# Deformable convolution after an edge-update block: patches of 14 by 8 pixels for two groups of 4 by 4 sample positions

## The chip, the cores and the metric

One core of a Trainium2 chip. The metric is the device time of one execution in microseconds (us), the median of several. TensorE (PE) multiplies matrices into PSUM, VectorE (DVE) and ScalarE (ACT) move and change data, GpSimd (POOL) does too but reaches SBUF only, SyncE (SP) issues DMAs.

## The reference

`x` is (2, 128, 128, 128), float32. Two layers are each added to their input:

```python
x = x + _L0_conv_ref(_gn(x), Wa, ba, Wb, bb, Wg, bg, Wo, bo)   # sigmoid(gate) * (a @ b), then @ Wo
x = x + _L1_conv_ref(_gn(x), w_off, b_off, w_def)

def _L1_conv_ref(x, w_off, b_off, w_def):
    x = jax.nn.relu(x)
    offset = conv(x, w_off, 3x3, padding 1) + b_off       # 18 channels: dy, dx for each of 9 taps
    py, px = base_y + off[:, :, 0], base_x + off[:, :, 1]  # 9 sample positions a pixel
    samp = _bilinear_gather(x, py, px)                     # zero outside the image
    return einsum('bckhw,ock->bohw', samp, w_def)
```

The change is in the second layer.

## The kernel before, in words

**First stage (to about 330 us).** 64 groups of rows go through layer one; the sum goes to DRAM as `x1_pad`, with a margin. Constant tables are loaded by SP in small pieces on the way.

**Band stage.** The image is cut into 64 bands of 8 rows by 64 columns. Sampling is a matrix product: for a window of 5 centre columns, all sample positions lie in a patch of 14 by 9 = 126 pixels (offsets up to 2 pixels). The patch, turned so that pixels lie on partitions, is PE's stationary operand (`zT`), and the moving one is `weights` (126 pixels by 9 taps by 40 positions): the product of a vertical and a horizontal hat function of the distance of each pixel to each position. A band has 66 centre columns of 8 (528 positions a tap), 14 windows and 13 steps. Each band passes these stages, and each engine runs them in the order of the table `ORDER`, in which a letter names the stage and a fixed lead in bands:

- `h` (3 bands ahead): ACT normalises the near pixels (L971) and rounds them to f16 (L959), DVE makes the low parts `z_lo` (L1324). `O`: PE convolves them to offsets (L824: nine products with `z_hi`, nine with `z_lo`), which leaves four partial sums on four groups of partitions; ACT adds the bias and takes them out (L982, `offs4`). `P`: DVE casts them to f16 (L1288) and subtracts (L1291), the split. `Q`, `locate`: PE selects and adds the partial sums and the constants for every (patch row, tap) and (patch column, tap) (L762 high, L764 low, for each axis), ACT takes the absolute value (L991, `dist`). `G`: DVE makes `hats` (L1299). `H`: ACT issues the stores of the hats to DRAM (L997). `R`: DVE reduces the reach (L1304).
- SP, `spread_hats`: each third (3 taps) of a band's hats is read back and broadcast, hat_y over the 9 patch columns, hat_x over 12 of the patch rows, into `hy_all` and `hx_all` (L564, 108 partitions by 1536 columns each). There is one buffer of each, so the loads of a third wait until POOL's three products of the band before with that third are done.
- `k` (1 ahead): POOL multiplies `hy_all` and `hx_all` into `weights` (L1570, nine products of 512 columns a band). `weights` has two buffers; the first product of a band waits until all sampling of the band before last is done.
- `z`, `T` (2 and 1 ahead): ACT makes the patches (L948), PE turns the 14 windows four at a time (L796), ACT and DVE copy them out in turns (L1015, L1334).
- `s`: PE samples (L778, 9 by 40 columns a step; float32, so each product is two passes), ACT copies the step to `samples_hi` in f16 (L1005), DVE makes `samples_lo` (L1314). There are three PSUM banks, so step p waits until the low parts of step p - 3 are done. Step 0 waits for all of the band's weights.
- `c` (1 behind): PE convolves (L750: three products of 512 columns a tap), DVE adds x (L1349), SP stores y.

## Time and profile before

| | |
|---|---|
| median of 3 runs (lowest, highest) | 1680.81 us (1674.68, 1682.14) |
| profiled execution: own time; span | 1692.53; 1690.7 us |
| PE busy; VectorE; ScalarE; GpSimd | 1543.5; 1096.4; 990.7; 941.8 us |
| TensorE's mean granted clock | 0.962 of full |
| DMA, mean over the span | 211 GB/s |
| hy_all and hx_all loads | 192 each, 648.0 KB each |
| chain that ended last, largest shares | DMA 42%, PE 23%, POOL 16% |

The span is what the trace covers; the own time of the profiled execution holds a little more, and both lie above the median of the runs. Busy PE time comes from modelled ends of pipelined matmuls, so the start of the next instruction tells the price of one better than its duration does. A reader takes the distance between starts where nothing waits. In rows, `L` is the line of the kernel, the first number the start, the second the length, and brackets give the idle time before and what ended it.

### The profile page before, as it was taken

What the parts mean: (1) busy time and instruction counts of PE and PEld (TensorE: products, weight loads), DVE (VectorE), ACT (ScalarE), POOL (GpSimd) and SP (SyncE); (2) the same over time, 40 slices, a digit from 0 to 9 for tenths busy, and PEclk for the clock granted to TensorE, in tenths of its full rate; (3) what the DMA queues carried; (4) which work ended last, traced back from release to release, by engine and by line L of the source; (5) the groups of instructions that cost most, each with busy time, mean ns of one, the idle gap of its engine ahead of it and who ended that gap; (6) DMA issues with size and microseconds to landing.
All of it is one profiled execution on the core that took longest, in us unless ns stands there. A gap on an engine that the chain in (4) does not pass through costs nothing.

```text
span 1690.7 us, 24883 instructions
## 1 busy us (share of the span) xinstructions
PE 1543.5 (91%) x8339; PEld 910.3 (54%) x8340; DVE 1096.4 (65%) x1964; ACT 990.7 (59%) x1564; POOL 941.8 (56%) x747
## 2 busy tenths in 40 slices
PE   6999999748998999989999999899999999889997
PEld 4777777514554555444554555455445554445554
DVE  6888888645666676565665666657556656556663
ACT  3555555435665666665666666557556666556662
POOL 4555555535565565555555655565556655556652
PEclk9999999858999999999999999999999999999999
DMA  5334333347777777777777777877787778777762
GB/s 149 116 117 116 116 115 112 120 145 250 235 253 247 244 259 236 235 230 236 244 230 240 237 256 246 235 239 240 238 249 247 267 230 247 219 235 251 253 243 68
DMA packets 145855, 356.90 MB, mean 211 GB/s; under 512 B 10875, under 2 KB 77976, under 8 KB 145752
## 3 DMA queue, kind: packets, MB, share of 16 engines
q1 hardware_dynamic: 131032, 328.46, 62.8%
q10 hardware_dynamic: 14720, 27.14, 4.6%
q8 instruction: 56, 0.92, 0.2%
q14 instruction: 47, 0.39, 0.1%
HBM read 292.42 MB, written 63.13 MB: 210 GB/s over the span
## 4 chain that ended last, share of the span: by engine, by line
DMA 42%; PE 23%; POOL 16%; issue 11%; DVE 3%; SPq 2%; ACT 1%; ACTq 0%; POOLq 0%; DVEq 0%
DMA hx_all<-hat_x 38%; POOL weights L1570 10%; PE bank L778 9%; PE pair L750 7%; POOL samples_hi L1519 4%; DMA hat_x<-hats 4%; PE pair L824 3%; SPq L564 2%; POOL rstd L1494 1%; PE pair L796 1%; POOL samples_lo L1506 1%; DVE hats L1299 1%; PE bank L796 1%; PE pair L762 1%; PE pair L764 1%
## 5 line engine op out<-in xcount | busy, mean ns | idle before, releaser
L1570 POOL TENSOR_TENSOR weights<-hy_all,hx_all 126x512 f32<-126x512 f32 x576 | 759.4, 1347 | 570.0 <-DMA hx_all<-hat_x 530.3
L1314 DVE SCALAR_TENSOR_TENSOR samples_lo<-bank,samples_hi 128x360 f16<-128x360 f32 (+1 forms) x832 | 434.1, 536 | 432.1 <-ACT samples_hi L1005 419.0
L778 PE MATMUL bank<-weights,zT 126*128 126x360 f32 (+1 forms) x1792 | 637.3, 474 | 78.1 <-POOL weights L1570 74.7
L1005 ACT ACTIVATE samples_hi<-bank 128x360 f16<-128x360 f32 (+1 forms) x832 | 385.4, 475 | 431.4 <-PE bank L778 405.0
L778 PEld LDWEIGHTS bank<-weights,zT 126*128 126x128 f32 x1792 | 314.8, 196 | 239.1 <-POOL weights L1570 79.7
L750 PE MATMUL pair<-samples_hi,w_hi 128*128 128x512 f16 x576 | 221.7, 385 | 1.3 <-DVE samples_lo L1314 1.3
L750 PE MATMUL pair<-samples_hi,w_lo 128*128 128x512 f16 x576 | 220.0, 382 | 0.0
L750 PE MATMUL pair<-samples_lo,w_hi 128*128 128x512 f16 x576 | 219.3, 381 | 0.0
L1506 POOL TENSOR_TENSOR samples_lo<-samples_hi,samples_lo 128x512 f16<-128x512 f32 x64 | 74.2, 1159 | 130.8 <-ACT samples_lo L909 130.7
L900 ACT ACTIVATE samples_hi<-pair,nbias,rstd 128x512 f32<-128x512 f32 x64 | 49.8, 778 | 148.5 <-PE pair L649 97.0
L948 ACT ACTIVATE z<-raw,norm_band 128x1764 f32<-128x1764 f32 (+3 forms) x80 | 132.1, 1671 | 0.0
L971 ACT ACTIVATE abg_space<-raw,norm_band 128x660 f32<-128x660 f32 (+2 forms) x74 | 101.9, 1391 | 17.2 <-DMA raw<-x_pad 11.8
L750 PEld LDWEIGHTS pair<-samples_hi,w_lo 128*128 128x128 f16 x576 | 57.2, 99 | 99.2 <-issue 69.4
L1299 DVE TENSOR_SCALAR hats<-dist 128x1024 f32<-128x1024 f32 x64 | 64.7, 1011 | 61.7 <-ACT dist L991 61.7
L824 PE MATMUL pair<-z_hi,woff 128*64 128x512 f16 x576 | 87.5, 412 | 15.9 <-ACT z_hi L959 15.9
L1015 ACT COPY zT<-pair 126x512 f32<-126x512 f32 x128 | 75.0, 586 | 37.1 <-PE pair L796 32.7
L750 PEld LDWEIGHTS pair<-samples_hi,w_hi 128*128 128x128 f16 x576 | 56.8, 99 | 71.4 <-issue 5.3
L750 PEld LDWEIGHTS pair<-samples_lo,w_hi 128*128 128x128 f16 x576 | 56.1, 97 | 70.8 <-issue 3.3
L991 ACT ACTIVATE dist<-pair 128x1024 f32<-128x1024 f32 x64 | 65.6, 1025 | 37.1 <-PE pair L764 37.1
L1519 POOL TENSOR_TENSOR samples_hi<-weights,all_o 128x512 f32<-128x512 f32 x64 | 81.5, 1275 | 0.0
L796 PEld LDWEIGHTS pair<-ident,z 128*126 128x126 f32 x512 | 64.8, 142 | 26.3 <-issue 2.1
L796 PE MATMUL pair<-ident,z 128*126 128x128 f32 x512 | 78.1, 276 | 0.0
(138 smaller groups left out, 1920.5 us busy)
## 6 DMA issues: line engine op xcount, KB each, us to landing
hy_all<-hat_y SPq DMA_DIRECT2D x192, 648.0 KB
hx_all<-hat_x SPq DMA_DIRECT2D x192, 648.0 KB
raw<-x_pad SPq DMA_DIRECT2D x68, 276.0 KB, 14.6
x_pad<-hy_all SPq DMA_DIRECT2D x64, 276.0 KB, 3.7
weights<-in_x SPq DMA_DIRECT2D x64, 256.0 KB, 3.0
out<-y SPq DMA_DIRECT2D x32, 512.0 KB, 13.5
hat_y<-hats ACTq DMA_DIRECT2D x64, 252.0 KB
hat_x<-hats ACTq DMA_DIRECT2D x64, 162.0 KB
```

The costliest lines, as they stand in the source:

```text
L750: mm = nc.tensor.matmul(bank[B_CONV], w_part[:, k, :], part[:, u, k, k % 3 * BR:k % 3 * BR + BW], start=(k == 0 and (w_part, part) == (w_h ...
L778: mm = nc.tensor.matmul(sampled_step(n, p)[:, :, c0 - first:c1 - first], zT[0:WPIX, u * WINDOWS + w, :], weights[0:WPIX, u, :, c0:c1], sta ...
L796: mm = nc.tensor.transpose(bank[B_ZT[g % 2]][0:WPIX, (w % 4) * P:(w % 4 + 1) * P], z[:, u, w].rearrange("p r c -> p (r c)"), ident[:])
L824: mm = nc.tensor.matmul(bank[B_OFF][at:at + width, :].rearrange("p (w r) -> p w r", r=BR), woff[:, k, 0:width], pixels[:, kx:kx + UW, ky:k ...
L948: done = nc.scalar.activation(z[:, u, :, rows, :], patches, ACT.Relu, bias=norm_band[:, 1].rearrange("p b n -> p (b n)")[:, n:n + 1], scal ...
L971: done = nc.scalar.activation(z_near[:, :, r0:r1], raw[:, src:src + r1 - r0, left:left + UW + 2].rearrange("p r w -> p w r"), ACT.Relu, bi ...
L1005: nc.scalar.activation(samples_hi[:, u, :, c0:c1], sampled_step(n, p), ACT.Copy).then_inc(samples_ready, 1)
L1299: nc.vector.tensor_scalar(hats[:], dist[:], -1.0, 0.0, ALU.add, ALU.min).then_inc(hats_ready, 1)
L1314: nc.vector.scalar_tensor_tensor(out=samples_lo[:, u, :, c0:c1], in0=sampled_step(n, p), scalar=1.0, in1=samples_hi[:, u, :, c0:c1], op0=A ...
L1506: nc.gpsimd.tensor_tensor(xT_lo[:], xT[:], xT_hi[:], ALU.subtract).then_inc(xT_lo_ready, 1)
L1519: nc.gpsimd.tensor_tensor(x_bo[:, s % 2, :].rearrange("p (f w) -> p f w", f=GC), xg[:, s, :].rearrange("p (f w) -> p f w", f=GC), all_o[:] ...
L1570: nc.gpsimd.tensor_tensor(weights[0:WPIX, u, k, at:at + BW], hy_all[0:WPIX, k, :], hx_all[0:WPIX, k, :], ALU.mult).then_inc(weights_ready, 1)
```

## The change

The patch becomes 14 by 8 pixels (112 partitions), a window 4 centre columns. Each patch serves two groups of 4 by 4 positions, the upper and lower half of the band, so every product samples 2 x 9 x 16 = 288 columns; a band has 17 windows and 16 steps. `hats`, `weights`, `hy_all`, `hx_all` and the banks hold the halves one behind the other. Each half needs 8 of the 14 patch rows, so a load writes 64 partitions. A band's loads are six pieces (half, 3 taps) in two DMAs each, 768 columns wide, and POOL makes one product of 3 x 256 columns for each. hat_y lies in DRAM twice per row (`COPIES`). The stores of the hats move from ACT's queue to SP's, behind the loads, and are six. The partial sums are first added two and two: ACT takes out partitions 64 on with bias (`offs_far`), DVE adds those from 0 on (`offs_sum`, a new instruction), and high and low parts then lie in one tensor (`offs_parts`), so that `locate` is one product an axis. `ORDER` is rewritten. The rest of the diff, left out below, lays constants out for this (eight more small loads in the first stage) and keeps the path for far offsets.

```diff
-BR, WC, UW = 8, 5, 64
+BR, WC, UW = 8, 4, 64
+HR = BR // 2
...
-CW = CENTERS * BR
+CW = CENTERS * HR
-WIN = WC * BR
+WIN = WC * HR
-NEAR_R = BR + 2 * REACH
+NEAR_R = HR + 2 * REACH
+COPIES = 2
...
+HALF = BW // 2
+CHUNK = TROWS * HALF
+PIECES = 2 * TAPS // TROWS
...
-            "h0 s0 s1 s2 k0 h1 c0 c1 T0 k1 s3 s4 z0 z1 O0 k2 s5 s6 P0 c2 c3 T1 k3 s7 s8 c4 k4 c5 s9 Q0 "
-            "c6 k5 G0 T2 s10 k6 H0 c7 k7 s11 c8 T3 k8 s12 R0").split()]
+            "h0 s0 s1 s2 k0 h1 c0 c1 s3 s4 T0 k1 z0 z1 O0 s5 s6 P0 k2 c2 c3 s7 s8 T1 c4 k3 c5 s9 s10 "
+            "Q0 k4 c6 G0 T2 s11 s12 c7 k5 T3 s13 s14 c8 T4 s15 R0").split()]
...
                 sp.wait_ge(*hats_landed(n))
-                for g in range(TROWS):
-                    wait(sp, weights_ready, TAPS * (n - 1) + TROWS * (g + 1))
...
+                for i in range(PIECES):
+                    h, g = divmod(i, TROWS)
+                    wait(sp, weights_ready, PIECES * (n - 1) + i + 1)
...
+                    sp.dma_start(
+                        hy_flat[rows, columns],
+                        hat_y[n % AHEAD, g, top * COPIES:(top + NEAR_R) * COPIES, h]
...
+            def store_hats(n):
+
+                sp.wait_ge(hats_ready, n + 1)
+                for h in range(2):
+                    columns = slice(h * HALF, (h + 1) * HALF)
+                    for copy in range(COPIES):
+                        sp.dma_start(
...
+                            hats[0:Y_ROWS, 0, columns]).then_inc(hat_out[n % AHEAD], 16)
+                    sp.dma_start(
...
                 if n + 2 < BANDS:
                     spread_hats(n + 2)
+                if n + AHEAD < BANDS:
+                    store_hats(n + AHEAD)
...
                 for axis in range(2):
-                    nc.tensor.matmul(pairs[0][:, axis, :], select[:, axis, :],
-                                     offs_hi[:], start=True, stop=False)
-                    mm = nc.tensor.matmul(pairs[0][:, axis, :], select[0:CONST_AT, axis, :],
-                                          offs_lo[0:CONST_AT, :], start=False, stop=True)
+                    mm = nc.tensor.matmul(pairs[0][:, axis, :], select[:, axis, :],
+                                          offs_parts[:], start=True, stop=True)
...
                 dve.wait_ge(off_evicted, n + 1)
+                wait(dve, off_split, n)
+                nc.vector.scalar_tensor_tensor(
+                    out=offs_sum[0:SUMS, :], in0=bank[B_OFF][0:SUMS, :],
+                    scalar=unscale[0:SUMS, OFF:OFF + 1], in1=offs_far[0:SUMS, :],
+                    op0=ALU.mult, op1=ALU.add).then_inc(off_summed, 1)
...
-            def weigh(n, u, k):
+            def weigh(n, u, i):
+
+                pool.wait_ge(hat_in[i], 32 * n + 32)
+                if i == 0:
                     wait(pool, sampled, STEPS * (n - 1))
...
+                             ap=[first.ap[0], [CW + HR, TROWS], [1, HALF]])
+                nc.gpsimd.tensor_tensor(to, hy_all[0:WPIX, i * TROWS:(i + 1) * TROWS, :],
+                                        hx_all[0:WPIX, i * TROWS:(i + 1) * TROWS, :],
+                                        ALU.mult).then_inc(weights_ready, 1)
```

VectorE, from the low parts `z_lo` to the hats. Before:

```order
L1324 TENSOR_TENSOR z_lo<-abg_space,z_hi 128x660 [waits z_hi_ready]
L1314 SCALAR_TENSOR_TENSOR samples_lo<-bank,samples_hi 128x9x40 [waits samples_ready] x4
L1288 CAST offs_hi<-offs 114x512 [waits located,off_evicted]
L1291 TENSOR_TENSOR offs_lo<-offs,offs_hi 114x512 [waits off_high]
L1334 COPY zT<-bank 126x512 [waits sampled,z_turned]
L1314 SCALAR_TENSOR_TENSOR samples_lo<-bank,samples_hi 128x9x40 [waits samples_ready] x3
L1299 TENSOR_SCALAR hats<-dist 128x1024 [waits hat_out0,dist_ready]
```

The same place after the change:

```order
L1379 TENSOR_TENSOR z_lo<-abg_space,z_hi 128x660 [waits z_hi_ready]
L1369 SCALAR_TENSOR_TENSOR samples_lo<-bank,samples_hi 128x18x16 [waits samples_ready] x4
L1337 SCALAR_TENSOR_TENSOR dist<-pair,unscale,dist 50x512 [waits off_split,off_evicted]
L1343 CAST offs_parts<-dist 50x512 [waits located,off_summed]
L1346 TENSOR_TENSOR offs_parts<-dist,offs_parts 50x512 [waits off_high]
L1369 SCALAR_TENSOR_TENSOR samples_lo<-bank,samples_hi 128x18x16 [waits samples_ready] x2
L1389 COPY zT<-bank 112x512 [waits sampled,z_turned]
L1369 SCALAR_TENSOR_TENSOR samples_lo<-bank,samples_hi 128x18x16 [waits samples_ready] x2
L1354 TENSOR_SCALAR hats<-dist 128x1024 [waits hat_out1,dist_ready]
```

The split has a sum ahead of it, and the low parts of steps 7 and 8 now stand directly behind it, ahead of the copy of windows.

PE, the sampling steps ahead of `locate`. Before, from the sixth product of the convolution on:

```order
L750 MATMUL pair<-samples_lo,w_hi 128x512
L778 MATMUL bank<-weights,zT 128x360 [waits lows_ready]
L762 MATMUL pair<-offs_hi,select 128x512 [waits dist_ready,off_split]
L764 MATMUL pair<-offs_lo,select 128x512
L762 MATMUL pair<-offs_hi,select 128x512
L764 MATMUL pair<-offs_lo,select 128x512
L750 MATMUL pair<-samples_hi,w_hi 128x512
```

After:

```order
L799 MATMUL pair<-samples_lo,w_hi 128x512
L828 MATMUL bank<-weights,zT 128x288 [waits lows_ready] x2
L812 MATMUL pair<-offs_parts,select 128x512 [waits dist_ready,off_split]
L812 MATMUL pair<-offs_parts,select 128x512
L799 MATMUL pair<-samples_hi,w_hi 128x512
```

Two steps, 9 and 10, stand ahead of `locate` where one stood, and the second of them needs the low parts of step 7.

## Rows read from the trace of the kernel before

**Rows 1.** Windows view: us, busy us (instructions) per engine, PEclk, DMA share, GB/s.

```profile
400.00:1040.00 640.00, 604.39 (x2850) 323.99 (x2850) 405.31 (x661) 400.87 (x640) 369.32 (x281) 0.98 0.78 242
```

**Rows 2.** Chain that ended last, 800 to 845 us: start, us, what.

```profile
822.86 16.92 DMA hx_all<-hat_x
```

**Rows 3.** Waits view, PE and POOL, 400 to 1680: us, times, longest.

```profile
PE bank L778 <- POOL weights L1570: 71.3, 31, 7.9
...
POOL weights L1570 <- DMA hx_all<-hat_x: 486.8, 172, 9.9
```

**Rows 4.** Source view of L1349, the addition of x: xcount, min/median/max ns, first, last start.

```profile
L1349 DVE SCALAR_TENSOR_TENSOR y<-pair,unscale,raw x74: 274/742/744, 421.7 to 1683.9; 128x512 f32<-128x512 f32 x54, 128x320 f32<-128x320 f32 x6, 128x192 f32<-128x192 f32 x6, 128x64 f32<-128x64 f32 x4
```

**Rows 5.** Timeline of PE, 1108.5 to 1129: start, us, engine line op xcount.

```profile
1108.29 1.32 PE L824 MATMUL pair<-z_hi,woff 128*64 128x512 f16 x9
...
1111.66 0.38 PE L750 MATMUL pair<-samples_hi,w_hi 128*128 128x512 f16 x1
...
1112.96 0.60 PE L796 MATMUL bank<-ident,z 128*126 128x128 f32 x4
1113.39 1.38 PE L778 MATMUL bank<-weights,zT 126*128 126x360 f32 x4
1114.61 0.38 PE L750 MATMUL pair<-samples_hi,w_hi 128*128 128x512 f16 x1
...
1121.20 3.08 PE L778 MATMUL bank<-weights,zT 126*128 126x360 f32 x10
1124.12 0.38 PE L750 MATMUL pair<-samples_hi,w_hi 128*128 128x512 f16 x1
...
1127.16 1.32 PE L824 MATMUL pair<-z_hi,woff 128*64 128x512 f16 x9
```

**Rows 6.** Timeline of PE, then of POOL, around 441 us.

```profile
440.24 2.20 PE L778 MATMUL bank<-weights,zT 126*128 126x360 f32 x8
...
441.33 3.74 POOL L1570 TENSOR_TENSOR weights<-hy_all,hx_all 126x512 f32<-126x512 f32 x3 [5.04 <-PE bank L778]
```

**Rows 7.** Source views of L1545 and L1570: xcount, min/median/max ns.

```profile
L1545 POOL TENSOR_TENSOR w_lo<-weights,w_hi x1: 2381/2381/2381, 307.6 to 307.6; 128x1152 f16<-128x1152 f32 x1
L1545 POOL TENSOR_TENSOR woff<-weights,woff x1: 496/496/496, 309.9 to 309.9; 128x162 f16<-128x162 f32 x1
...
L1570 POOL TENSOR_TENSOR weights<-hy_all,hx_all x559: 1254/1273/1972, 399.7 to 1660.4; 126x512 f32<-126x512 f32 x187
```

**Rows 8.** Timeline, 1120.5 to 1141, then source views of L1291 and L1314.

```profile
1122.74 0.61 DVE L1314 SCALAR_TENSOR_TENSOR samples_lo<-bank,samples_hi 128x432 f16<-128x432 f32 x1 [0.19 <-ACT samples_hi L1005]
...
1124.83 4.35 POOL L1570 TENSOR_TENSOR weights<-hy_all,hx_all 126x512 f32<-126x512 f32 x3 [6.37 <-DMA hx_all<-hat_x]
...
1125.92 0.88 DVE L1324 TENSOR_TENSOR z_lo<-abg_space,z_hi 128x660 f16<-128x660 f32 x1
...
1130.64 4.35 POOL L1570 TENSOR_TENSOR weights<-hy_all,hx_all 126x512 f32<-126x512 f32 x3 [1.46 <-DMA hx_all<-hat_x]
...
1131.68 0.51 DVE L1288 CAST offs_hi<-offs 114x512 f16<-114x512 f32 x1
...
1132.22 1.64 DVE L1291 TENSOR_TENSOR offs_lo<-offs,offs_hi 114x512 f16<-114x512 f32 x1
...
L1291 DVE TENSOR_TENSOR offs_lo<-offs,offs_hi x64: 691/693/1762, 345.6 to 1621.5; 114x512 f16<-114x512 f32 x64
...
L1314 DVE SCALAR_TENSOR_TENSOR samples_lo<-bank,samples_hi x832: 515/533/609, 382.7 to 1676.7; 128x360 f16<-128x360 f32 x154, 128x432 f16<-128x432 f32 x13
```

**Rows 9.** Timeline of PE at its first sampling step.

```profile
380.59 2.17 PE L778 MATMUL bank<-weights,zT 126*128 126x360 f32 x3 [3.36 <-POOL weights L1570]
```

**Rows 10.** Timelines of ScalarE's and SP's queues, first band's hats and a later load.

```profile
350.70 0.27 ACTq L997 DMA_DIRECT2D hat_x<-hats  x1
...
353.65 0.85 SPq L564 DMA_DIRECT2D hy_all<-hat_y  x1
...
1131.46 0.76 SPq L564 DMA_DIRECT2D hy_all<-hat_y  x1
```

More of the change, by code:

```diff
@@ L241, in preact_conv_kernel @@
         parts = sb("parts", [P, BW], BF16)
-        offs, rest = hy_all[0:NOFF, 0], hy_all[0:NOFF, 1]
-        row_in, row_z, row_zT = (hy_all[:, 2, i * P:(i + 1) * P] for i in range(3))
-        far_dist, far_hats, far_weights = hx_all[:, 0:2], hx_all[:, 2:4], weights[:, 1, 0, 0:BW]
-        samples = weights[:, 0, :, 0:BW]
+        offs, rest = hy_far[0:NOFF, 0], hy_far[0:NOFF, 1]
+        row_in, row_z, row_zT = (hy_far[:, 2, i * P:(i + 1) * P] for i in range(3))
+        far_dist, far_hats = hx_far[:, 0:2], hx_far[:, 2:4]
+        samples, far_weights = (weights[:, i].rearrange("p k c -> p (k c)")[:, 0:TAPS * BW]
+                                .rearrange("p (k c) -> p k c", k=TAPS) for i in range(2))
+        far_weights = far_weights[:, 0]
         in_f32 = sem("in_f32")
@@ L398, in sampled_step @@
             first, end = step_columns(p)
-            return (bank[B_S[(STEPS * n + p) % 3]][:, 0:TAPS * (end - first)]
-                    .rearrange("p (k c) -> p k c", k=TAPS))
+            return (bank[B_S[(STEPS * n + p) % 3]][:, 0:2 * TAPS * (end - first)]
+                    .rearrange("p (k c) -> p k c", k=2 * TAPS))
         def by_column_tap(tile):
@@ new lines, in store_hats @@
+            def store_hats(n):
+                sp.wait_ge(hats_ready, n + 1)
+                for h in range(2):
+                    columns = slice(h * HALF, (h + 1) * HALF)
+                    for copy in range(COPIES):
+                        sp.dma_start(
+                            hat_y[n % AHEAD].rearrange("g (r o) h c -> (g r) o h c", o=COPIES)
+                            [:, copy, h].rearrange("a (k c) -> a k c", k=TROWS),
+                            hats[0:Y_ROWS, 0, columns]).then_inc(hat_out[n % AHEAD], 16)
+                    sp.dma_start(
+                        hat_x[n % AHEAD].rearrange("r g h c -> (r g) h c")
+                        [:, h].rearrange("a (k c) -> a k c", k=TROWS),
+                        hats[0:X_ROWS, 1, columns]).then_inc(hat_out[n % AHEAD], 16)
@@ L571, in _ @@
             sp.wait_ge(hats_cleared, 2)
-            spread_hats(0)
-            spread_hats(1)
+            for n in range(AHEAD):
+                store_hats(n)
+                if n + 1 < AHEAD:
+                    spread_hats(n)
             for n in range(BANDS + 2):
@@ L769, in sample @@
                 if p == 0:
-                    wait(pe, weights_ready, TAPS * (n + 1))
+                    wait(pe, weights_ready, PIECES * (n + 1))
                 if p % 4 == 0:
@@ L991, in distances @@
                 nc.scalar.activation(dist[:], pairs[0][:], ACT.Abs).then_inc(dist_ready, 1)
-            def store_hats(n, u, _):
-                wait(act, hats_ready, n + 1)
-                for axis, rows in enumerate((Y_ROWS, X_ROWS)):
-                    act.dma_start(hat_rows[axis][n % AHEAD].rearrange("g r (k c) -> (g r k) c", k=TROWS),
-                                  hats[0:rows, axis, :]).then_inc(hat_out[n % AHEAD], 16)
             def copy_samples(n, u, p):
@@ L1344, in add_x1 @@
                 whole = min(BR, RING * RB - at)
-                for r0, r1, src in ((0, whole, at), (whole, BR, 0)):
-                    if r0 == r1:
-                        continue
-                    added = nc.vector.scalar_tensor_tensor(
-                        out=y[:, b % 2, :].rearrange("p (r w) -> p r w", r=BR)[:, r0:r1,
-                                                                              left:left + UW],
-                        in0=bank[B_CONV].rearrange("p (w r) -> p r w", r=BR)[:, r0:r1],
-                        scalar=unscale[:, DEF:DEF + 1],
-                        in1=raw[:, src:src + r1 - r0, MARGIN + left:MARGIN + left + UW],
-                        op0=ALU.mult, op1=ALU.add)
+                to = y[:, b % 2, :].rearrange("p (r w) -> p r w", r=BR)
+                of = bank[B_CONV].rearrange("p (h w r) -> p h r w", h=2, r=HR)
+                for h in range(2):
+                    cut = min(max(whole - h * HR, 0), HR)
+                    for r0, r1 in ((0, cut), (cut, HR)):
+                        if r0 == r1:
+                            continue
+                        src = (at + h * HR + r0) % (RING * RB)
+                        added = nc.vector.scalar_tensor_tensor(
+                            out=to[:, h * HR + r0:h * HR + r1, left:left + UW],
+                            in0=of[:, h, r0:r1], scalar=unscale[:, DEF:DEF + 1],
+                            in1=raw[:, src:src + r1 - r0, MARGIN + left:MARGIN + left + UW],
+                            op0=ALU.mult, op1=ALU.add)
                 added.then_inc(y_ready, 1)
```

150 lines of the change are left out of this document (85 added, 65 removed).

## Prediction, made before the changed kernel ran

> **What bounds the kernel now.** I read the busy time by stretch first, then the chain, the waits, and one band instruction by instruction. In the band stage TensorE (PE) is busy 604 of 640 us while VectorE, ScalarE and GpSimd (POOL) stand at 405, 401 and 369 [rows 1]: PE is nearly the bound. Yet the chain that ended last runs for bands on end through a load of hx_all, 16.92 us of it in a band, and the products that wait for it [rows 2]. The waits join the two: POOL waits 486.8 us for hx_all, in 172 pieces, and hands on only 71.3 us to PE, in 31 [rows 3]. The mean band is (1683.9 - 421.7) / 63 = 20.03 us [rows 4]. A band without a wait for POOL takes PE from 1108.29 to 1127.16, 18.87 us [rows 5]. So loads that come late cost 1.16 us a band, the waits and the lower clock in some bands (0.98 granted on the mean [rows 1]) together. **No more than 73 us can be had this way, and what the new band costs comes off it.**
>
> **PE's own stream.** The sampling products have 9 x 528 = 4752 columns a band before and 18 x 264 = 4752 after, so that price stays; the convolution has the same 27 products of 512 columns. Added: three window turns, at (1113.39 - 1112.96) / 4 = 0.11 each, +0.33 [rows 5]. Removed: two of four 512-column products of `locate`; six such products take 1112.96 - 1111.66 = 1.30, so -0.43 [rows 5]. At the seam of two bands the last step and the first three of the next take 1124.12 - 1121.20 = 2.92 us [rows 5]; their columns (eight full passes at (1114.61 - 1113.39) / 4 = 0.30 each, two to a step, and two short ones, 0.12) fill some 2.53. PE waits 0.39 there: the third step's bank is freed 1.59 us after the last step's end. The new last step has the same 432 columns, but the two steps ahead of the third shrink from 0.60 to 0.48 each, so the wait grows to 0.63: +0.24. Sum 18.87 + 0.33 - 0.43 + 0.24 = 19.0 us for a PE that waits for nothing else.
>
> **The loads.** A band's loads shrink from 6 x 108 rows of 6144 bytes (4.0 MB) to 12 x 64 rows of 3072 (2.4 MB), and each of six pieces is freed by its own product. In a band of 20 us the transfers that took 17 us for a third of 4.0 MB, with the rest beside it, have time to land: I count POOL's wait for loads at nothing. What covers it is a whole band between the issue of a piece and its use.
>
> **What is late next: POOL against VectorE.** POOL then starts its products as soon as the buffer is free, 0.37 us after the last sampling step (440.24 + 0.72 = 440.96 to 441.33) [rows 6], and runs all six in a row. Call that step's end zero. One product of 3 x 256 columns is not in the trace. The one of 512 takes 1273 ns. A product with one half-size operand takes 496 ns for 162 columns and 2381 for 1152, thus 1.90 ns a column and 0.19 us fixed [rows 7]. Floor: 1.27 + 256 x 1.90 = 1.76 us; ceiling: 1.5 x 1.27 = 1.91. I take 0.19 + 1.5 x 1.08 = 1.81, nearest to the row of the same types, less 0.04 of overlap (three stand in 3.74 us, not 3.82 [rows 6]): 1.775 apart. Whether three rows of 256 in one product cost more than one of 768 no row shows; the ceiling holds 0.05 us for each of the two. The Trainium skill, page GPSIMD Engine Reference, section Elementwise — side-by-side cycle accounting, counts about 2.6 cycles of 1.2 GHz an element for a product of two inputs; an estimate by it is 1.83 us, 0.1 us more a band and 6 us more in all.
>
> POOL and VectorE get in each other's way. The cast of the split began at 1131.68 during a product that ended at 1131.91, and ended 0.28 after it; the subtraction behind it took 1.64 us instead of 0.69 [rows 8]. The other way round, `z_lo` at 1125.92 stretched the three products from 1124.83 on to 4.35 instead of 3.74, by 0.61 [rows 6, 8]. The subtraction's median is 693 ns and its longest 1762 [rows 8], so in most bands no product was in its way; now one is in every band. `z_lo` asks at 1125.92 - 1121.92 = 4.0, or 3.8 with shorter copies ahead, near the end of the second product. So POOL ends at 0.37 + 6 x 1.775 + 0.04 + 0.61 = 11.67. The cast came at 1131.68 - 1121.92 = 9.76 [rows 8]; shorter steps ahead take 0.24 off and the new sum of partial offsets, one input in PSUM like `y`'s 0.74, adds as much as that [rows 4] (bounds: nothing, if VectorE were idle there, and 0.74 + 0.2 for latency). It asks at 10.26, after the sixth product has begun at 9.86. **It waits for that product.** Cast done at 11.95, subtraction 11.99 to 12.68, then the low parts of step 7, which may begin 0.08 before the end: 533 ns for 360 columns and 609 for 432 make 0.46 for 288 [rows 8], to 13.06. Step 10 needs that bank, 0.17 us later (the seam shows 1123.35 to 1123.52): **13.23**. Its place in PE's order is 12.35 (seam to the third step's end 2.07; then seven steps at 0.48, six taps of the convolution at 0.65, two turns of four windows at 0.44, and the offsets' convolution 1111.66 - 1108.29 less two steps, 2.15), so PE waits 0.9 us. From there to the band's end stand five steps of 0.48 and the last of 0.72, three taps 1.94, nine turns 0.98 and `locate` 0.43: 6.49 with the rounding. Band: 13.23 + 6.49 = **19.72**. With products from floor to ceiling (1.72 to 1.87 apart) 19.4 to 20.0; at the ceiling the cast slips in ahead of the sixth product and only the subtraction waits.
>
> **Outside the bands.** PE's first sampling step waited 3.36 us for POOL's first products [rows 9]; smaller pieces end that: -3.4. Eight more small loads in the set-up, at the 0.76 us that SP takes for a load [rows 10], come while SP is ahead of the first groups: 0, up to +6. Two halves of the last addition, extra copy of windows, longer patches for ScalarE: VectorE and ScalarE have 35% free, and every wait on them falls inside the 0.9 us that PE waits anyway; were that gone they would cost some 0.2.
>
> **Sum.** 63 x (19.72 - 20.03) = -19.5, and -3.4: -23 us against the profiled execution (span 1690.7, its own time 1692.5, 0.7% over the median). On the median of 1680.8 that is **1658 us**. For the products' bounds: 1638 to 1677. A measurement of this kernel can tell about 0.5% (8 us) from no change.
>
> **Rivals.**
> 1. *PE alone is the bound*: the cast gets through, because products are shorter or start earlier than I think. 19.0 a band, 1680.8 - 65 - 3 = 1613. For it: PE has no other wait in a clean band. Against: the products would have to stand 1.63 apart, below my floor. 0.12.
> 2. *SP's queue becomes the loop* (the slower side). Stores leave ScalarE and go to SP, six instead of two. The loop is: stores landed, twelve loads issued, stores issued, landed. A load's issue takes 0.76, and the first loads began 353.65 - 350.97 = 2.7 us after the stores' issue [rows 10]. With stores at the 0.76 of a load the loop is 9.1 + 4.6 + 2.7 and 0.9 for `raw` and `y`: 17.3, under the band. At the 0.27 of the old store it is 14.3. From 1.2 us a store it decides; at 1.3 it is 20.5 and the time 1680.8 + 30 - 3 = 1707. For it: stores in rows of 3 x 256 are new here, so no row prices them. Against: 2.4 us to spare. 0.15.
> 3. *The loads are hidden no better*: shorter rows, the second copy of hat_y's rows and 648 store rows instead of 207 eat the gain, POOL still waits, and the change does not do what it says. Then the band stays near 20.03, with the new cost of PE (+0.13) 1680.8 + 8 - 3 = 1685. For it: the transfers are shared out in order. Against: 40% fewer bytes at the same 242 GB/s [rows 1]. 0.15.
>
> **Chances.** Forecast 0.58 (0.50 of it faster, 0.08 same), PE alone 0.12 (faster), SP 0.15 (0.13 slower, 0.02 same), loads 0.15 (0.10 same, 0.05 slower). Faster 0.62, same 0.20, slower 0.18. Range 1630 to 1700: it reaches most of the way to both outer cases and leaves out about 0.1 on each side.
>
> **What would show it.** Right: POOL's wait for hx_all falls from 487 us to near nothing and its wait for PE's sampling takes the place; six products in a row from 0.4 to 11.7 us after the last step; cast and subtraction of the split behind the sixth; PE waiting about 0.9 us for samples_lo at step 10 and 0.6 at step 2 in every band; the granted clock near 1.00 in the bands. Wrong: a product far from 1.8 us, a split that ends before the sixth product, waits of POOL for loads, or SP's loads issued later than the products that free their place.

## The result, and the profile after

The changed kernel takes 1656.14 us (median of 4 runs, 1655.2 to 1658.35), the one before 1679.61 (4 runs, 1674.68 to 1682.14): a ratio of 0.9866, 95% interval 0.984 to 0.9891. It is faster, by 1.3%, and 2 us from the forecast. As shown below, part of that closeness is luck. Ratios and intervals in this document use only the runs within 1.5% of the fastest of their kernel. 54 more runs of the kernel before, made beside the experiments below, have a median of 1673.3 us, and six of them lie below 1656.1: against those the change is worth 1.0%, and not in every execution. The profiled execution has its own time of 1655.2 and a span of 1653.1 us.

The windows view of the same stretch as [rows 1]: span of the stretch, then busy us and instructions of PE, PEld, DVE, ACT and POOL, then clock, DMA share and GB/s.

```profile
400.00:1040.00 640.00, 627.58 (x3160) 363.79 (x3159) 501.71 (x845) 441.13 (x790) 366.65 (x195) 1.00 0.63 183
```

PE is busy 628 of 640 us in place of 604, at a granted clock of 1.00 in place of 0.98, and the DMA engines move 183 GB/s in place of 242. The waits view, 400 to 1640 us (us in total, times, longest), answers to [rows 3]:

```profile
POOL weights L1629 <- PE bank L828: 513.8, 61, 8.8
...
PEld pair L874 <- DVE z_lo L1379: 36.4, 58, 0.7
...
POOL weights L1629 <- DMA hx_all<-hat_x: 6.6, 3, 5.4
```

GpSimd waited 486.8 us for `hx_all`; now 6.6, and its wait for TensorE's sampling has taken the place. TensorE waits for no weights in this stretch. The loads are off the path, as forecast.

One band of TensorE, with the rows that say where it stands (timeline: start, length, what, idle time before and its releaser). It answers to [rows 5].

```profile
1099.87 1.61 PE L874 MATMUL pair<-z_hi,woff 128*64 128x512 f16 x9
...
1102.47 1.24 PE L828 MATMUL bank<-weights,zT 112*128 112x288 f32 x4
...
1107.55 1.45 PE L828 MATMUL bank<-weights,zT 112*128 112x288 f32 x4
1108.84 0.60 PE L812 MATMUL pair<-offs_parts,select 119*128 119x512 f16 x2
...
1114.15 1.87 PE L828 MATMUL bank<-weights,zT 112*128 112x288 f32 x8
1116.31 0.75 PE L828 MATMUL bank<-weights,zT 112*128 112x288 f32 x2 [0.29 <-DVE samples_lo L1369]
1116.90 0.38 PE L799 MATMUL pair<-samples_hi,w_hi 128*128 128x512 f16 x1
```

GpSimd, two bands (timeline): the distance of the starts, 19.82 us, is the band, and the six products take 11.3. The last row is from the source view of all 384 products: shortest, median and longest, in ns.

```profile
1095.37 11.34 POOL L1629 TENSOR_TENSOR weights<-hy_all,hx_all 112x768 f32<-112x768 f32 x6 [8.49 <-PE bank L828]
1115.19 7.76 POOL L1629 TENSOR_TENSOR weights<-hy_all,hx_all 112x768 f32<-112x768 f32 x4 [8.49 <-PE bank L828]
...
L1629 POOL TENSOR_TENSOR weights<-hy_all,hx_all x384: 1799/1822/2476, 368.3 to 1617.3; 112x768 f32<-112x768 f32 x192
```

The second row is cut off at the window's end. VectorE in the same band (timeline), to be read beside GpSimd's products, which end at 1095.37 + 11.34 = 1106.71:

```profile
1098.96 2.50 DVE L1379 TENSOR_TENSOR z_lo<-abg_space,z_hi 128x660 f16<-128x660 f32 x1
...
1104.57 0.73 DVE L1337 SCALAR_TENSOR_TENSOR dist<-pair,unscale,dist 50x512 f32<-50x512 f32 x1
1105.33 1.65 DVE L1343 CAST offs_parts<-dist 50x512 f16<-50x512 f32 x1
1107.02 0.69 DVE L1346 TENSOR_TENSOR offs_parts<-dist,offs_parts 50x512 f16<-50x512 f32 x1
1107.73 0.82 DVE L1369 SCALAR_TENSOR_TENSOR samples_lo<-bank,samples_hi 128x288 f16<-128x288 f32 x2
```

The cast begins at 1105.33 and ends at 1106.98, 0.27 after the sixth product. With no product beside it, it takes 0.42 (shown below). `z_lo` takes 2.50 in place of 0.8. Counted from the end of the last sampling step of the band before (1114.15 + 0.72 less a band, 1095.05), the forecast chain stands like this:

| us after the last step | forecast | measured |
|---|---|---|
| first product starts | 0.37 | 0.32 |
| sixth product ends | 11.67 | 11.66 |
| cast ends | 11.95 | 11.93 |
| subtraction ends | 12.68 | 12.66 |
| low parts of step 7 | 13.06 | about 13.1 |
| step 10 starts (0.48 before 1108.84) | 13.23 | 13.31 |
| step 10's own place in PE's order | 12.35 | 12.98 (1107.55 + 0.48) |
| from step 10 to the band's end | 6.49 | 6.51 |
| band | 19.72 | 19.82 |

### The profile page after: what moved, and what is told of

Its sections match the earlier page's. It is cut to its first block, busy times and chain, and to the rows that moved or that the text cites. A ratio compares the mean times of both kernels' runs of the same rounds, so it can differ in the third digit from the quotient of the medians.

```text
span 1653.1 us, 26938 instructions
## 1 busy us (share of the span) xinstructions
PE 1555.0 (94%) x8787; PEld 972.4 (59%) x8788; DVE 1271.9 (77%) x2283; ACT 1044.2 (63%) x1820; POOL 907.9 (55%) x555
## 4 chain that ended last, share of the span: by engine, by line
PE 60%; issue 13%; DVE 11%; POOL 7%; ACT 6%; SPq 2%; DMA 1%; POOLq 0%; DVEq 0%; ACTq 0%
PE bank L828 25%; PE pair L799 17%; PE pair L874 9%; POOL samples_hi L1577 4%; DVE samples_lo L1369 4%; PE pair L846 4%; DVE offs_parts L1343 3%; ACT samples_hi L1050 3%; PE bank L846 2%; PE pair L812 2%; ACT dist L1034 2%; DVE dist L1337 2%; POOL rstd L1552 1%; ACT z L999 1%; POOL samples_lo L1564 1%
## 5 line engine op out<-in xcount | busy, mean ns | idle before, releaser
L1629 POOL TENSOR_TENSOR weights<-hy_all,hx_all 112x768 f32<-112x768 f32 x384 | 724.3, 1922 | 556.4 <-PE bank L828 513.8
L828 PE MATMUL bank<-weights,zT 112*128 112x288 f32 (+1 forms) x2176 | 630.3, 410 | 25.9 <-DVE samples_lo L1369 23.2
L1050 ACT ACTIVATE samples_hi<-bank 128x288 f16<-128x288 f32 (+1 forms) x1024 | 409.5, 416 | 365.5 <-PE bank L828 337.8
L1369 DVE SCALAR_TENSOR_TENSOR samples_lo<-bank,samples_hi 128x288 f16<-128x288 f32 (+1 forms) x1024 | 445.9, 463 | 225.8 <-ACT samples_hi L1050 219.6
L828 PEld LDWEIGHTS bank<-weights,zT 112*128 112x128 f32 x2176 | 370.8, 190 | 206.4 <-DVE samples_lo L1369 127.8
L1379 DVE TENSOR_TENSOR z_lo<-abg_space,z_hi 128x660 f16<-128x660 f32 x64 | 148.4, 2319 | 5.3 <-ACT z_hi L1010 2.2
L999 ACT ACTIVATE z<-raw,norm_band 128x1904 f32<-128x1904 f32 (+3 forms) x80 | 131.2, 1660 | 0.0
L1060 ACT COPY zT<-pair 112x512 f32<-112x512 f32 (+1 forms) x192 | 91.9, 479 | 29.1 <-PE pair L846 23.5
L1343 DVE CAST offs_parts<-dist 50x512 f16<-50x512 f32 x64 | 96.2, 1504 | 2.2
L846 PE MATMUL pair<-ident,z 128*112 128x128 f32 x576 | 95.8, 276 | 0.0
```

What stands on the lines that cost most here:

```text
L828: mm = nc.tensor.matmul(sampled_step(n, p)[:, :, c0 - first:c1 - first], zT[0:WPIX, u * WINDOWS + w, :], weights[0:WPIX, u, :, c0:c1], sta ...
L846: mm = nc.tensor.transpose(bank[B_ZT[g % 2]][0:WPIX, (w % 4) * P:(w % 4 + 1) * P], z[:, u, w].rearrange("p r c -> p (r c)"), ident[:])
L999: done = nc.scalar.activation(z[:, u, :, rows, :], patches, ACT.Relu, bias=norm_band[:, 1].rearrange("p b n -> p (b n)")[:, n:n + 1], scal ...
L1050: nc.scalar.activation(samples_hi[:, u, :, c0:c1], sampled_step(n, p), ACT.Copy).then_inc(samples_ready, 1)
L1060: nc.scalar.copy(zT[0:WPIX, at:at + c, :].rearrange("p w c -> p (w c)"), bank[B_ZT[0]][0:WPIX, 0:c * P]).then_inc(zT_a, 1)
L1343: nc.vector.tensor_copy(offs_parts[0:SUMS, :], offs_sum[0:SUMS, :]).then_inc(off_high, 1)
```

## Where the 37 us of the two profiles lie

The profiled executions differ by 1690.7 - 1653.1 = 37.6 us, the medians by 23.5. The low parts of the last step, one a band (VectorE's timeline), count the bands. Before:

```profile
422.92 0.61 DVE L1314 SCALAR_TENSOR_TENSOR samples_lo<-bank,samples_hi 128x432 f16<-128x432 f32 x1 [0.19 <-ACT samples_hi L1005]
...
1629.77 0.61 DVE L1314 SCALAR_TENSOR_TENSOR samples_lo<-bank,samples_hi 128x432 f16<-128x432 f32 x1 [0.18 <-ACT samples_hi L1005]
...
1676.70 0.61 DVE L1314 SCALAR_TENSOR_TENSOR samples_lo<-bank,samples_hi 128x432 f16<-128x432 f32 x1 [0.17 <-ACT samples_hi L1005]
```

After:

```profile
421.81 0.61 DVE L1369 SCALAR_TENSOR_TENSOR samples_lo<-bank,samples_hi 128x432 f16<-128x432 f32 x1 [0.37 <-ACT samples_hi L1050]
...
1591.34 0.61 DVE L1369 SCALAR_TENSOR_TENSOR samples_lo<-bank,samples_hi 128x432 f16<-128x432 f32 x1 [0.37 <-ACT samples_hi L1050]
...
1639.92 0.61 DVE L1369 SCALAR_TENSOR_TENSOR samples_lo<-bank,samples_hi 128x432 f16<-128x432 f32 x1
```

From the second band's to the fourth from the last there are 59 intervals: (1629.77 - 422.92) / 59 = 20.46 us before, (1591.34 - 421.81) / 59 = 19.82 after; 59 x 0.64 = 37. The three bands at the end are another matter, since no offsets are left to be made: 46.9 us for three before, 48.6 after. Up to the first row of each, 1.1 us were gained, and behind the last row 0.8. 1.1 + 37.3 - 1.7 + 0.8 make the 37.6. **So a full band of the kernel before took 20.46 us, not the 20.03 of the prediction**, which had averaged in the three short bands and the 8 us behind them, in which only the last convolution and its additions are left.

## Experiments

Each kernel starts from the changed one unless its edit says otherwise. The kernel before, run beside them, lay between 1638.9 and 1701.9 us. It seems that how late its loads come varies from run to run: with lighter loads, in the last experiment but one, its four runs lie within 3.1 us. The changed kernel and its variants stay within some 0.3% of their medians (0.5% in the last experiment). So variants are compared by their medians, with the 1656.1 of the changed kernel, and by their bands; the changed kernel itself was not run again beside them. My theory: the chain sixth product, cast, subtraction, low parts of step 7, step 10 sets the band. The main rival: TensorE's own stream does.

### The sixth product held back for the split

```diff
+                if i == 5:
+                    pool.wait_ge(off_split, min(n + 3, BANDS))
```

> GpSimd's sixth product waits until the split of the offsets two bands ahead is done; nothing else is changed. In the changed kernel every band takes 19.82 us: the cast waits 1.2 us for the sixth product, so that step 10 starts 13.3 us after the last step of the band before. My theory (the chain sixth product, cast, subtraction, low parts of step 7, step 10 sets the band; the wait for z_lo ahead of it lies inside its time): cast asks at 10.3 us, gets SBUF at once, low parts are there at 11.9, step 10 starts at 12.98, where TensorE's own order has it with the wait for z_lo. Band 19.82 - 0.33 = 19.5, over 60 full bands -20 us: about 1636 us. Rival (TensorE's own stream takes 19.8 us, and the product is beside the point): no change, 1656. Rival (GpSimd has no time to give): it ends 1 us later than 11.7 of 19.8, the time rises.

1635.94 us (1635.25 to 1638.3), 59 full bands at 19.52 on the mean. VectorE's and GpSimd's timelines:

```profile
1016.24 0.42 DVE L1343 CAST offs_parts<-dist 50x512 f16<-50x512 f32 x1
...
1017.53 1.81 POOL L1631 TENSOR_TENSOR weights<-hy_all,hx_all 112x768 f32<-112x768 f32 x1 [1.68 <-DVE offs_parts L1346]
```

GpSimd's fifth product had ended 1.68 us before the sixth began, so the cast had no product beside it, and takes 0.42 us. A wait that was added, of 1.68 us on GpSimd, makes the kernel 20 us faster, because GpSimd is idle 8.5 us a band and the chain through it was not. TensorE's stream alone cannot explain that: it was not touched.

### The third product held back for z_lo

```diff
+                if i == 2:
+                    pool.wait_ge(z_lo_ready, min(n + 3, BANDS))
```

> GpSimd's third product waits until z_lo of the band two ahead is made; nothing else is changed. My theory: z_lo takes 0.8 us in place of 2.2 to 2.5, and TensorE no longer waits 0.45 us in the offsets' convolution. But the products end no earlier (about 11.8 us after the last step), the split still collides with the last of them, and step 10 still starts at 13.2 to 13.5: the wait moves there, the band stays at 19.7 to 20.0, the time within 1648 to 1668. Rival (the waits add up, each is worth its own length): band 19.82 - 0.45 = 19.4, 1629 us.

1671.5 us (1669.08 to 1674.43), median band 19.99, mean 20.09. VectorE's timeline:

```profile
1011.16 0.84 DVE L1379 TENSOR_TENSOR z_lo<-abg_space,z_hi 128x660 f16<-128x660 f32 x1
...
1017.40 0.42 DVE L1343 CAST offs_parts<-dist 50x512 f16<-50x512 f32 x1
1017.86 2.19 DVE L1346 TENSOR_TENSOR offs_parts<-dist,offs_parts 50x512 f16<-50x512 f32 x1
```

`z_lo` is short again, the cast slips in between two products, and the subtraction behind it runs into the sixth and takes 2.19. The chain ends 0.2 us later than before: a wait was taken away (PEld's wait for z_lo) and the kernel is 15 us slower. I had given 1648 to 1668: the median band lies in the range that I gave, but 18 of the 59 bands take 20.2 to 20.5, which I did not foresee. In these the sum and the cast come 0.2 to 0.5 us later, and in 15 of them the cast misses the gap between the products: it takes 1.93 to 1.96, and the subtraction 0.69. What makes the sum late there is open. That the waits add up is refuted.

### Both held back

> GpSimd's third product waits for z_lo and its sixth for the split, both of the band two ahead. My theory: both collisions are gone; GpSimd ends at about 13.0 us after the last step instead of 11.7, of 19 it has. TensorE is left with its own stream and the 0.6 us wait at the seam of two bands: band 19.0, over 60 bands -49 us: about 1607. That is more than the two alone give together (-20 and 0), since they lie one inside the other. Rival (TensorE's own stream is longer than I summed up, 18.4 of columns and turns and 0.6 at the seam): it stays above 19.4, 1630 or more.

1630.99 us (1630.34 to 1632.26), median band 19.40: **my number missed by 24 us**, and it is the rival of that text that holds. TensorE waits at the seam alone. By the forecast's own sum, from the start of a band's last step to the end of the next band's third takes 2.75 us (as in the changed kernel, 1114.15 to 1116.90), its columns 2.16, and 0.59 is lost there, 0.63 in the forecast. So TensorE's own stream is 19.4 us, not the 19.0 of the prediction. Its timeline shows where:

```profile
1008.65 1.61 PE L874 MATMUL pair<-z_hi,woff 128*64 128x512 f16 x9
1010.19 1.02 PE L874 MATMUL pair<-z_lo,woff 128*32 128x512 f16 x9
1011.14 1.24 PE L828 MATMUL bank<-weights,zT 112*128 112x288 f32 x4
```

Nine products with `z_hi` take 1.54 and nine with `z_lo` 0.95 us, 2.49 in all. In the kernel before the first nine began at 1108.29 [rows 5], and then:

```profile
1109.54 0.88 PE L824 MATMUL pair<-z_lo,woff 128*32 128x512 f16 x9
1110.35 1.48 PE L778 MATMUL bank<-weights,zT 126*128 126x360 f32 x4
```

That is 1.25 and 0.81 us. Products, columns and type are the same, and so is the granted clock of that band (1.00); the way the pixels are read is not. That led to the next two.

### The offsets' convolution reads in runs of 8 again

```diff
-                        bank[B_OFF][at:at + width, :].rearrange("p (h w r) -> p h w r", h=2, r=HR),
+                        bank[B_OFF][at:at + width, :].rearrange("p (h w r) -> p w h r", h=2, r=HR),
                         woff[:, k, 0:width],
-                        pixels[:, kx:kx + UW, ky:ky + BR].rearrange("p w (h r) -> p h w r", h=2),
+                        pixels[:, kx:kx + UW, ky:ky + BR].rearrange("p w (h r) -> p w h r", h=2),
```

On the changed kernel alone:

> The changed kernel with the 18 products of the offsets' convolution reading their pixels in runs of 8, as before, and writing the halves apart into PSUM, where the changed kernel reads in runs of 4 and writes in a row. Each such pair of products took 0.284 us after the change against 0.22 to 0.24 before, 0.35 us a band. My theory of the price: the short runs that are read slow the product; with runs of 8 the convolution is back at 2.1 us. My theory of the band: TensorE gets to step 10 that much earlier and waits that much longer there, since the sixth product and the split set it: 19.8 us a band and 1650 to 1658 us. Rival (TensorE's stream bounds): -0.35 a band, 1635.

And with both waits of GpSimd:

> GpSimd's third and sixth product wait for z_lo and the split (band 19.40 us, 1631 us), and the offsets' convolution reads in runs of 8. TensorE is the bound there, so here the 0.35 us count in full: band 19.05, 1610 us. If writing the halves apart into PSUM costs the same as reading short runs: 1631.

The first: 1654.18 us (1652.33 to 1656.88), median band 19.79. The second: 1609.42 (1608.75 to 1609.85), median band 19.02. TensorE's timeline of the first, then of the second (whose three rows give 1.28 and 0.84 us):

```profile
1003.40 0.91 PE L874 MATMUL pair<-z_lo,woff 128*32 128x512 f16 x9 [0.28 <-DVE z_lo L1379]
...
1009.31 1.55 PE L828 MATMUL bank<-weights,zT 112*128 112x288 f32 x4
1010.70 0.60 PE L812 MATMUL pair<-offs_parts,select 119*128 119x512 f16 x2
```

```profile
1016.29 1.35 PE L874 MATMUL pair<-z_hi,woff 128*64 128x512 f16 x9
1017.57 0.91 PE L874 MATMUL pair<-z_lo,woff 128*32 128x512 f16 x9
1018.41 1.24 PE L828 MATMUL bank<-weights,zT 112*128 112x288 f32 x4
```

18 products take 2.12 us in place of 2.49. The same 0.37 us are worth nothing where GpSimd's chain sets the band (they turn into a longer wait for `z_lo` and for step 10: its two steps take 1.39 to `locate`, 1.29 without the edit), and all of it, 19.40 to 19.02, where TensorE does. It is the cleanest test of what bounds the changed kernel, and it is needed: in a band of the changed kernel the view of the chain that ended last follows the long cast back to the sum ahead of it and to the convolution, and names no product of GpSimd, since no semaphore joins the cast to the product. By that chain alone, 0.37 us less of convolution would have shortened the band.

### The split behind the low parts of steps 7 and 8

```diff
-            "... O0 s5 s6 P0 k2 c2 c3 s7 s8 T1 c4 k3 ..."
+            "... O0 s5 s6 k2 c2 c3 s7 s8 P0 T1 c4 k3 ..."
```

> The order table alone is changed: the split of the offsets (sum, cast, subtraction) stands behind the low parts of steps 7 and 8 on VectorE, not ahead of them. My theory: the cast then asks at about 11.5 us, near the end of the sixth product, the low parts of step 7 no longer wait behind it, and step 10 starts at its place, 12.98; locate, 0.5 later, finds the split done at about 12.8. Band 19.5, about 1636 us, the same as with the sixth product held back. If it is instead locate, not step 10, that sets the band, the time stays at 1656.

1653.82 us (1652.48 to 1656.68), median band 19.79. Here the alternative of my text came true. From VectorE's and TensorE's timelines:

```profile
1007.56 0.42 DVE L1343 CAST offs_parts<-dist 50x512 f16<-50x512 f32 x1
1008.01 0.69 DVE L1346 TENSOR_TENSOR offs_parts<-dist,offs_parts 50x512 f16<-50x512 f32 x1
...
1007.51 1.14 PE L828 MATMUL bank<-weights,zT 112*128 112x288 f32 x4
1008.76 0.60 PE L812 MATMUL pair<-offs_parts,select 119*128 119x512 f16 x2
```

The cast no longer collides, step 10 no longer waits, but the sum now stands behind the low parts of step 8 and the split ends at 1008.70, right where `locate` wants it: `locate` starts 0.28 us late. The wait was moved from step 10 to the product behind it. I had put the end of the split at 12.8 after the last step; it is 13.7 (1008.70 less 995.01, where the last step of the band before ended), because the low parts of step 8 first wait for TensorE.

### The first turn of windows in the seam

```diff
-            "h0 s0 s1 s2 k0 h1 c0 c1 s3 s4 T0 k1 z0 z1 O0 ..."
+            "h0 s0 s1 T0 s2 k0 h1 c0 c1 s3 s4 k1 z0 z1 O0 ..."
```

Alone:

> The changed kernel with that turn moved into the seam and nothing else. By my theory the band is set by GpSimd's six products, the cast and the low parts behind them, which all count from the last sampling step, so that TensorE merely waits 0.4 us longer for step 10: 19.8 us a band, 1650 to 1658. If TensorE's stream bounds: 1630.

1655.12 us (1651.31 to 1656.47), median band 19.82: nothing, as expected. With both waits and runs of 8:

> As the kernel with both waits of GpSimd and reading in runs of 8 (1609 us, band 19.05), and with the first turn of four windows (0.44 us of TensorE) moved from behind step 4 to between steps 1 and 2, where TensorE waits 0.56 us at the seam of two bands. My theory: TensorE is the bound there, so the turn goes into the wait: band 18.65, 60 x 0.4 less, 1585. Against it: ScalarE then copies the turned windows (0.48 us) between the high copies of steps 1 and 2, which makes step 2's copy and the low parts behind it late for step 5, and could give back up to 0.4.

1604.18 us (1603.06 to 1606.19), median band 18.96. Of the 0.4 only 0.06 came. VectorE's timeline says where the rest went, and it is not step 2's copy, against which I had warned, though it is the same copy of turned windows on ScalarE:

```profile
1014.57 0.85 DVE L1379 TENSOR_TENSOR z_lo<-abg_space,z_hi 128x660 f16<-128x660 f32 x1 [0.18 <-ACT z_hi L1010]
...
1019.79 1.42 DVE L1343 CAST offs_parts<-dist 50x512 f16<-50x512 f32 x1
```

`z_lo` now waits for `z_hi`, which that copy holds up by 0.5 us, GpSimd's third to fifth products follow it later while TensorE is earlier, and the cast meets the fifth product. So the guard goes one product forward:

```diff
-                if i == 5:
+                if i == 4:
```

> The kernel with both waits, runs of 8 and the turn in the seam (1604 us, band 18.96), with GpSimd's wait for the split moved from ahead of its sixth product to ahead of its fifth. There, z_lo ended 0.5 us later (the copy of windows stands ahead of it on ScalarE), the fifth product with it, and the cast of the split hit it: 1.42 us in place of 0.42. My theory: the cast is again 0.42, step 10 no longer waits 0.3, GpSimd ends about 15 us after the last step of 18.6 it has. Band 18.65, 1585 us. Rival (GpSimd now ends too late for the next band's first step, or the copy on ScalarE is what costs): 1600 or more.

**1583.74 us** (1582.9 to 1585.76), median band 18.65, a ratio to the kernel before of 0.9502 (0.9448 to 0.9555). It is the fastest kernel here, and 4.4% faster than the change as it was made. The windows view and GpSimd's timeline:

```profile
400.00:1040.00 640.00, 640.00 (x3361) 390.37 (x3359) 453.59 (x896) 456.68 (x838) 371.09 (x207) 1.00 0.67 195
```

```profile
1002.47 3.59 POOL L1633 TENSOR_TENSOR weights<-hy_all,hx_all 112x768 f32<-112x768 f32 x2 [1.51 <-DVE z_lo L1379]
1007.99 3.60 POOL L1633 TENSOR_TENSOR weights<-hy_all,hx_all 112x768 f32<-112x768 f32 x2 [1.93 <-DVE offs_parts L1346]
1016.01 3.61 POOL L1633 TENSOR_TENSOR weights<-hy_all,hx_all 112x768 f32<-112x768 f32 x2 [4.42 <-PE bank L828]
```

TensorE is busy all of the stretch. GpSimd is held back twice a band and still waits 4.4 us for TensorE at the end.

### The kernel before with lighter loads

Here the kernel before loads 904 of the 1536 columns of each piece. The other columns of `hy_all` and `hx_all` are not refreshed, so part of the weights is made of old data.

```diff
-                        sp.dma_start(dst[g * SRC_C:(g + NEAR_R) * SRC_C,
-                                         g * CHUNK:(g + 1) * CHUNK],
-                                     src.broadcast_to([NEAR_R, SRC_C, CHUNK])
+                        sp.dma_start(dst[g * SRC_C:(g + NEAR_R) * SRC_C,
+                                         g * CHUNK:g * CHUNK + 904],
+                                     src[:, :, 0:904].broadcast_to([NEAR_R, SRC_C, 904])
```

> The kernel before with loads of hats cut from 1536 to 904 columns a piece (2.3 MB a band in place of 4.0, as much as the changed kernel loads); the columns left out are not refreshed, so their products are of old data; nothing else is changed, the work of every engine is the same. It measures what late loads cost the kernel before. In its trace the 60 full bands take 20.46 us on the mean, 18.87 the undisturbed ones. My theory: nearly all of the difference is the loads; GpSimd waits for TensorE instead, a band takes 18.9 to 19.2, the time falls by 60 x 1.3 to 1.6, to about 1590 (1580 to 1610), well below the changed kernel. Rival (GpSimd's nine products in a row then hit the split as in the changed kernel): about 19.6 a band, 1625.

1587.7 us (1585.43 to 1588.56), a ratio of 0.9579 (0.9439 to 0.9719); every full band takes 18.87. So late loads cost the kernel before 92 us of its median of 1680 (88 of the 1676.0 that it took beside this run), and every band is back at the 18.87 us of an undisturbed one when the bytes are cut. The changed kernel cuts as many bytes and is 68 us above this one: that is what the new band costs, 59 x (19.82 - 18.87) = 56, 2 in the three last bands, and about 9 up to the end of the second band's sampling. GpSimd's products stand in a row here too, and the cast and the subtraction collide with them (source views):

```profile
L1288 DVE CAST offs_hi<-offs x64: 426/1436/1520, 344.4 to 1516.7; 114x512 f16<-114x512 f32 x64
...
L1291 DVE TENSOR_TENSOR offs_lo<-offs,offs_hi x64: 693/1639/1662, 344.8 to 1517.9; 114x512 f16<-114x512 f32 x64
```

Both take 1.0 us more than alone, and no band is longer for it. The order before placed step 10 and its low parts behind `locate`; the new order placed step 10 ahead of it. The collision is not what is new, but that somebody waits for its end.

### SyncE's stores twice

```diff
+                for to_y, to_x in ((hat_y, hat_x), (spare_y, spare_x)):
-                for h in range(2):
+                    for h in range(2):
...
```

> The changed kernel with every store of hats made twice, the second time to a spare tensor in DRAM: six more stores a band on SyncE's queue, 4.9 us a band, and 0.4 MB more. It tests the rival that SyncE's queue would be the loop. By the loop as my prediction summed it (stores landed, twelve loads, stores, landed) a band would be 7.5 of loads, 9.8 of stores, 2.7 of landing and 1.8 for the rest, 21.8 us: 1656 + 120 = 1776. By the trace, in which the hats of three bands ahead are stored and SyncE waits over 4 us a band for GpSimd and for the hats, the queue needs 19.1 of 19.8 us and nothing comes late: no change, 1656, at most 1670.

1677.63 us (1675.57 to 1686.36). 21 us slower than the changed kernel: not the 120 of the prediction's loop, but more than the 14 I had allowed. The loads wait until the spare stores have landed too. SyncE's timeline of the changed kernel, then of this one:

```profile
1107.34 0.66 SPq L594 DMA_DIRECT2D hx_all<-hat_x  x1
1111.25 1.66 SPq L605 DMA_DIRECT2D hat_y<-hats  x2
```

```profile
1116.41 1.67 SPq L610 DMA_DIRECT2D hat_y<-hats  x2
...
1125.43 0.76 SPq L614 DMA_DIRECT2D spare_x<-hats  x1
1128.00 0.57 SPq L592 DMA_DIRECT2D hy_all<-hat_y  x1
```

In the changed kernel SyncE stands still 3.2 us between its last load and the first store. With twelve stores it does not: the first store follows the last load within 0.1 us. It stands still at another place, behind the last store, and the waits view of SyncE's queue (400 to 1640 us; changed kernel, then this one) says for what:

```profile
SPq L588 <- DMA hat_x<-hats: 40.7, 36, 4.6
```

```profile
SPq L592 <- DMA spare_x<-hats: 65.3, 37, 3.2
```

SyncE waits for its own stores to land. It issues the stores of band n + 3 in one round and reads them back at the start of the next, so the landing is a part of its loop, as the prediction had it; my text for this experiment had left it out. The round is 7.9 us of loads and 9.8 of stores, and then either 1.9 for `y` and `raw`, in every other band, or a wait of 1.8 (1126.19 to 1128.00) for the last store: 19.5 to 19.7 us of 19.8 in both cases. The loop of the prediction gave 21.8 since it took 2.7 for the landing and added `y` and `raw` to it, which are issued while the stores land. 35 of the 59 bands still take 19.8, others up to 21.5 (mean 20.06), and GpSimd waits for `hx_all` again, 140.8 us in 37 pieces. So SyncE's round becomes the bound at about twice the stores of the change. What share of the late loads comes from the added bytes (the stretch from 400 to 1040 moves 210 GB/s in place of 183), and not from the round, is not separated.

## Why the prediction was right, and where it was not

- **The loads.** Right. POOL's wait for `hx_all` went from 487 to 7 us, the clock in the bands from 0.98 to 1.00.
- **POOL against VectorE.** Right to 0.1 us in every row of the table above but that of TensorE's own order (next point), and shown as a cause: holding the sixth product back gives the 20 us that the chain says. The product of 3 x 256 columns takes 1.82 us (1.81 forecast), three rows of 256 cost no more than the columns do, and the estimate of 1.83 from the Trainium skill (page GPSIMD Engine Reference, section Elementwise — side-by-side cycle accounting) is as good here. `z_lo` stretched a product by 0.65 (2476 ns in place of 1822), where I had 0.61.
- **PE's own stream: 19.0.** Wrong, it is 19.4. The prediction said nothing of the offsets' convolution, since neither products nor columns change, and reading in runs of 4 instead of 8 adds 0.37 us (shown by the two kernels with runs of 8). The step that failed is `12.35`, step 10's place: it is 12.98, of which 0.34 is the convolution, 0.11 the wait for `z_lo` (2.60 against 2.49) and 0.2 where products follow a turn or the convolution. It did not touch the band, since all of it lies ahead of a wait: TensorE waits 0.33 us at step 10, not 0.9.
- **The mean band: 20.03.** Wrong, and this is the largest miss. The sum set a full band after, 19.72, against a mean before that held the three short ones and the drain at the end [rows 4]; a full band took 20.46. By the trace's own time the sum was then 60 x (19.72 - 20.46) - 3.4 = -48, to 1645, and the profiled execution came to 1655.2. The median hid this: the profiled execution of before was 12 us above it, and those 12 us were in all likelihood late loads too (with lighter loads the kernel before hardly varies), which the change takes away whatever their size. On the median, (1680.8 - 1692.5) / 60 off the band makes 20.26, and 60 x (19.82 - 20.26) = -26, to 1654. The forecast of 1658 is the sum of a baseline 0.43 us too short and a run 0.7% too slow, which cancel.
- **Outside the bands: -3.4.** Not there. TensorE's first sampling step starts at 380.26 in place of 380.59 [rows 9]: the wait for weights is gone, but the offsets' products and turns ahead of it end later by as much.
- **Rivals.** PE alone did not come (19.82, not 19.0), but is what GpSimd's waits make of it. SyncE's queue is no bound: it stands still 3.2 us a band for the hats. A load takes 0.6 us to issue where the rival had 0.76, a store 0.8, and the landing costs about 1.6 (1.8 with the doubled stores) where it had 2.7, with `y` and `raw` inside it. The loop that the rival named is there, as the doubled stores show; its sum was too long. The loads were hidden.

## What to carry to other kernels

Take both sides of a difference from the same kind of stage, full steady bands against full steady bands, never a mean with the drain in it, and ask whether what the change removes is what makes the profiled run differ from the median. Where two engines exclude each other in SBUF, the one with slack can be made to wait: a semaphore wait on an idle engine at the right product was worth 20 us here, while 0.37 us a band of work taken from TensorE was worth nothing until such waits were in. Each guard must be placed for the times at which the operations then come. And read a layout change through to every reader: a product with the same columns may read them in shorter runs.

## What the runs showed of the hardware

- A product of TensorE with 512 columns of f16 read in runs of 4 elements (8 bytes) is slower than one in runs of 8: 0.95 us for nine against 0.84, and 1.54 against 1.28 for the wider ones. Writing the 512 results to PSUM in runs of 4 float32, with the halves 1 KB apart, cost 0.03 us for nine at most: 0.84 and 1.28, where the kernel before, writing in a row and reading in runs of 8, takes 0.81 and 1.25. The Trainium skill, page SBUF — State Buffer, section Door 1: The DMA port swizzle, says that SBUF gives full bandwidth for accesses that stay within a line of 16 bytes; by that rule runs of 8 bytes, which change the line more often, should be slower, and the trace agrees in direction. The same place says that any non-contiguous pattern in PSUM slows products significantly; for runs of 16 bytes the trace shows 2 to 4%.
- The cast and the subtraction, when they come during a product of GpSimd, end 0.14 to 0.15 us less than their own length after that product: the cast (0.42 alone) 0.27 behind it, the subtraction (0.69 alone) 0.55 behind it (1020.05 against 1019.50, with the third product held back). The product of GpSimd that meets `z_lo` is longer by less than `z_lo` takes alone (0.65 for 0.78 to 0.85). The same page, section Who interferes with whom, calls the ports that the two engines share a lock for a whole instruction; these rows agree.
- The addition of partial offsets (L1337), with one input in PSUM, took 732 to 744 ns in all 64 cases, 0.73 also where products ran beside it: it does not wait for them, while the cast and the subtraction, from SBUF alone, do.
